# An attention and FFN layer on eight cores: 53 tiles of exponentials on VectorE in place of 43, and a new planner of the order of work

## The reference, cut to what matters

```python
# x: 4 x 4096 x 1024; 16 heads of queries (64 wide), one head of keys and values
x = x + attention(layernorm(x))
x = x + ffn(layernorm(x))

def attention(r):
    q = einsum('bnd,hkd->bnhk', r, query_proj)
    k = r @ key_proj                       # one key head for all 16
    v = r @ value_proj
    sim = einsum('bnhk,bmk->bnhm', q, k) / sqrt(64)
    o = einsum('bnhm,bmv->bnhv', softmax(sim), v)
    return einsum('bnhv,dhv->bnd', o, output_proj)

def ffn(x):
    s = x @ Win + bin_                     # 1024 -> 64
    h = relu(s[..., None] * W1 + b1)       # 16 per unit
    g = sum(h * W2, -1) + b2
    return g @ Wout + bout
```

## Time and profile before

| | |
|---|---|
| median of three runs | 975.62 us |
| the profiled execution, its own time | 975.78 us |
| its span, slowest core | 974.2 us |
| spans of the eight cores | 972.4 to 974.2 us |
| ScalarE busy | 913.7 us, 94% |
| TensorE matmul busy | 896.4 us, 92% |
| VectorE busy | 649.2 us, 67% |

### The profile page before, as it was taken

How to read it: one execution, slowest core, us unless ns; L and a number is a source line. 1 busy time by engine, 2 the same in 40 slices (tenths; PEclk the granted TensorE clock), 3 DMA queues, 4 the chain that set the end, 5 groups by cost and what they waited for, 6 DMA issues and landing times.

```text
span 974.2 us, 29152 instructions; the slowest of 8 cores (972.4 to 974.2 us)
## 1 busy us (share of the span) xinstructions
PE 896.4 (92%) x11484; PEld 479.6 (49%) x11484; DVE 649.2 (67%) x938; ACT 913.7 (94%) x1000; POOL 77.0 (8%) x150
## 2 busy tenths in 40 slices
PE   4799899999999999999999999999999998998884
PEld 3345555555445545554555455554544454444441
DVE  4545666662438987878888878778852368828725
ACT  2579999999999999999999999999999999999971
POOL 3201121220000001000010000000010000100000
PEclk9999999999999999999999999999999999999995
DMA  9602244550110200000130000100040010421101
GB/s 208 139 14 88 89 107 119 125 132 2 21 26 8 26 9 13 19 7 7 51 130 14 18 18 13 18 8 28 30 136 18 18 24 7 134 64 18 50 2 43
DMA packets 46291, 48.71 MB, mean 50 GB/s; under 512 B 35152, under 2 KB 35280, under 8 KB 46160
## 3 DMA queue, kind: packets, MB, share of 16 engines
q1 hardware_dynamic: 38352, 27.71, 11.1%
q0 software_dynamic: 7520, 18.62, 7.4%
q10 hardware_dynamic: 288, 0.52, 0.1%
HBM read 35.70 MB, written 8.39 MB: 45 GB/s over the span
## 4 chain that ended last, share of the span: by engine, by line
ACT 81%; issue 11%; PE 4%; DVE 2%; DMA 1%; POOL 0%; DVEq 0%; SPq 0%; POOLq 0%; ACTq 0%
ACT ptu L1082 81%; PE ob L646 1%; DMA xbuf<-x_own 1%; DVE lnst L668 0%; PE spa L911 0%; DVE lnst L672 0%; PE sdb L579 0%; PE spb L948 0%; PE spb L911 0%; POOL rstd L1105 0%; DVE qt L745 0%; DVE r1u L691 0%; ACT hz L1092 0%; PE sda L568 0%; DVE gacc L1052 0%
## 5 line engine op out<-in xcount | busy, mean ns | idle before, releaser
L1082 ACT ACTIVATE ptu<-spa 128x1024 bf16<-128x1024 f32 x491 | 560.3, 1141 | 15.9 <-PE spa L911 15.5
L1082 ACT ACTIVATE ptu<-spb 128x1024 bf16<-128x1024 f32 x490 | 560.6, 1144 | 0.6 <-PE spb L911 0.5
L646 PE MATMUL ob<-vab,ptu 128*128 128x65 bf16 x7848 | 390.5, 195 | 1.0 <-DVE vab L742 0.6
L646 PEld LDWEIGHTS ob<-vab,ptu 128*128 128x128 bf16 x7848 | 285.4, 97 | 199.5 <-issue 199.5
L911 PE MATMUL spa<-qt,k2t 64*128 64x512 bf16 x982 | 192.9, 381 | 26.4 <-ACT ptu L1082 17.8
L911 PE MATMUL spb<-qt,k2t 64*128 64x512 bf16 x980 | 192.2, 380 | 20.7 <-ACT ptu L1082 19.4
L911 PEld LDWEIGHTS spa<-qt,k2t 64*128 64x128 bf16 x982 | 57.9, 92 | 116.1 <-issue 103.3
L911 PEld LDWEIGHTS spb<-qt,k2t 64*128 64x128 bf16 x980 | 59.0, 92 | 112.8 <-issue 99.4
L978 DVE TENSOR_TENSOR oacc<-oacc,ob 128x520 f32<-128x520 f32 x52 | 36.2, 696 | 71.7 <-PE ob L646 71.3
L1103 POOL TENSOR_SCALAR lnve<-lnmv 128x1 f32<-128x1 f32 x48 | 17.9, 374 | 561.1 <-DVE lnmv L674 561.1
L841 DVE SCALAR_TENSOR_TENSOR r1t<-oacc 128x1024 bf16<-128x1024 f32 x43 | 52.6, 1224 | 5.6 <-DVE oacc L836 5.2
(11 more groups left out here) (139 smaller groups left out, 729.1 us busy)
## 6 DMA issues: line engine op xcount, KB each, us to landing
xbuf<-x_own SPq DMA_DIRECT2D x16, 512.0 KB, 5.8
xbuf<-x_oth SPq DMA_DIRECT2D x16, 512.0 KB, 3.8
out<-xbuf POOLq DMA_DIRECT2D x14, 512.0 KB, 3.0
xbuf<-x_own POOLq DMA_DIRECT2D x12, 512.0 KB, 7.2
wqb<-wq POOLq DMA_DIRECT2D x8, 256.0 KB, 6.3
xtra<-x_own SPq DMA_DIRECT2D x4, 512.0 KB, 4.8
xtra<-wp POOLq DMA_DIRECT2D x8, 256.0 KB, 4.5
ot<-on SPq DMA_TRANSPOSE x38, 2.3
```

The costliest lines, as they stand in the source:

```text
L646: r = te.matmul(osum[:, hd, c * 65:(c + 1) * 65], ptu[:, g % NPT, hd * 512 + c * 128:hd * 512 + (c + 1) * 128], vab[:, CHUNKS[s][i], :], s ...
L1082: sc.activation(ptu[:, g % NPT, :], sps[g % 2][:], AF.Exp, scale=0.125 / SCORE_SCALE).then_inc(ex, 1)
```

## The change

1. `OFF` takes 53 tiles from ScalarE, in place of 43: 19, 19 and 15 for k = 1, 2, 3, in place of 17, 17 and 9. The last segment has four, where it had one.
2. `pace` is written anew. It keeps a clock for each engine and a time for every exponential (`exp_at`), plays VectorE's streams in order of time by priority, and lets a TensorE piece in only if it ends before the next scores are due. VectorE has six streams: `out_side` (was `o_out`) and `key_norm_side` (the norms of tiles 4 to 31, which were part of the evacuations) are added, and its block now just follows one list `order`.
3. The opening: `phase_a_order` has the queries of pairs 1 and 2 before the transposes; the statistics of tiles 2 and 3 come one norm earlier; ScalarE doubles `wkb` after its first copy, not before; one query weight is loaded a tile earlier.

```diff
-OFF = {1: [1, 2, 3, 2, 3, 2, 2, 2], 2: [2, 2, 3, 2, 2, 2, 2, 2], 3: [2, 0, 0, 2, 1, 2, 1, 1]}
+OFF = {1: [2, 3, 2, 3, 2, 2, 2, 3], 2: [2, 3, 4, 3, 2, 2, 1, 2], 3: [2, 1, 1, 3, 1, 0, 3, 4]}
...
-    o = [("V", 0, 0)] + q(0, 1) + tr[:1] + q(0, 2) + tr[1:2] + q(0, 3) + tr[2:3] + q(0, 4) + tr[3:]
-    o += [("V", 1, 0)] + q(0, 5, 6, 7)
+    o = [("V", 0, 0)] + q(0, 1, 2) + tr[:2] + q(0, 3) + tr[2:] + q(0, 4) + [("V", 1, 0)] + q(0, 5, 6, 7)
...
-SWITCH = 20
+SWITCH = 10
...
+MARGIN = 4
...
+    def run_dve(w):
+        clock["dve"] = max(clock["dve"], ready_at(head[w][0])) + head[w][1]
+        order.append(w)
         head[w] = next(sides[w], None)
...
+            force(want, "s")
+            clock["pe"] = max(clock["pe"] + SWITCH * (mode[0] != "halves"), exp_at[g] + EXPED)
+            exp_at[g + 2] = max(exp_at[g + 1] + SLOT, clock["pe"] + SCORED)
+            clock["pe"] += SCORES
...
+            off = [j for j in range(done["epv"], len(OFF_TILES)) if OFF_TILES[j][0] == s]
+            if off and not (6 <= r and ok([("exv", off[0] + 1)], clock["pe"]) or r >= n - 1 - len(off)):
+                off = []
+            off_at[g] = off[:1]
+            force(want + [("exv", j + 1) for j in off[:1]], "v")
...
+            limit = exp_at[g + 2] + SLOT - SCORED - MARGIN if g + 2 in exp_at else 1 << 40
...
+            end = start + PIECE + SWITCH * (mode[0] != ("whole" if whole else "halves")) + SWITCH * whole
+            if g + 3 < NG and not open_end:
+                limit = max(limit, ready_at(wanted(g + 3)) - 2)
+            if end > limit and not (open_end and start <= clock["pe"]):
+                break
...
         def _(v):
 
             ln_stats(v, 0)
             ln_stats(v, 1)
             ln_norm(v, 0)
+            ln_stats(v, 2)
             ln_norm(v, 1)
-            ln_stats(v, 2)
+            ln_stats(v, 3)
             ln_norm(v, 2)
-            ln_stats(v, 3)
             ln_norm(v, 3)
...
+            for w in order:
+                next(sides[w], None)
...
-            sc.wait_ge(wkl, 16)
-            sc.activation(wkb[:, :, 64:128], wkb[:, :, 0:64], AF.Copy).then_inc(wkd, 1)
...
+                if step == 0:
+                    sc.wait_ge(wkl, 16)
+                    sc.activation(wkb[:, :, 64:128], wkb[:, :, 0:64], AF.Copy).then_inc(wkd, 1)
...
-                for c in {2: [1], 3: [2], 4: [3], 5: [4], 6: [5], 7: [6], 8: [7]}.get(i, []):
+                for c in {2: [1], 3: [2, 3], 4: [4], 5: [5], 6: [6], 7: [7]}.get(i, []):
```

391 lines of the change are left out of this document (222 added, 169 removed).

## The result

The change makes the kernel slower: 980.1 us (median), beside 975.7 before; the ratio of after to before is **1.0046, with a 95% interval of 1.0032 to 1.0061**. Forecast were 972.9 us. 980.1 lies just inside the range given, on the wrong side of no change.

The account below looks back on a forecast made before the run. ScalarE was taken to set the pace at 0.919 us per exponential, besides the opening and the end. From the profiled 975.78: -9.2 + 1.5 - 8.2 - 1.8 + 14.8 = -2.9, so 972.9 us, range 965.5 to 981.

Parts of the forecast that it names:

- Ten exponentials, -9.2: ScalarE gets 971 tiles in place of 981, at 0.919 us each: 9.2 us less if ScalarE stays the bound.
- From k = 1 on, +1.5: From k = 1 on, VectorE's added load makes some evacuations late: 1.5 us more, between zero and 11.
- nothing prices one: From k = 1 on: the old trace has no late evacuation, so their cost was taken between zero and 11 us.
- the 4 at which it called itself wrong: From k = 1 on: at most 2 us of ScalarE waits on scores expected; wrong if more than 4.
- The opening, -8.2: Up to exponential 16: earlier start and fewer waits put it at 47.3, from 55.55, 8.2 us less.
- the walk: Step-by-step reckoning of TensorE and VectorE through the first 16 slots: first exponential near 24.5, then waits of 8.1 us.
- thinnest margin: In the opening, the second of five query-weight loads issued earlier must land by 27.9 us.
- Near 100 us, -1.8: Near 100 us: a 1.4 wait and 0.4 of short steps go, as slab 2's keys finish two slots earlier.
- The end, +14.8: Behind X, the last exponential's start: late off tiles put `zrec` at X + 16.1, 14.3 us more, plus 0.5 for the clock.
- I take 0.5 us for that: In the end: cost allowed for TensorE's clock falling while it is nearly idle for six us, 0.5 us.
- Rival (a): In the end: clock down when the last off tile is ready, costing 1.3 and 1.2 more, 974.9 us; chance 0.12.
- Against: it did work until X + 5: In the end: argument against (a), that TensorE worked until 5 us after the last exponential's start, X.

Follow-up runs that it names:

- e8: The changed kernel with each tile of x asked for again as soon as its own store is done, not after the group's last: 979.0 us.
- e7: The changed kernel with the scores computed twice in slots from k = 1 on where TensorE has nothing else: 980.9 us.
- e2: The changed kernel with the old table of 43 off tiles, so the new planner and opening alone: 969.9 us.
- e4: The changed kernel with 12 and 30 unread matmuls on TensorE ahead of its waits for the last two off tiles' exponentials: 977.3 us.

## Why the prediction was wrong, by its steps

- **Ten exponentials, -9.2: right.** The pace stayed 0.919, and VectorE at 89% in k = 1 and 2 held no one back. A tile cost VectorE 6.7 us (66.7 for ten) and not 7.6.
- **From k = 1 on, +1.5: measured +3.2 on the slowest core, +1.9 on the mean, by another mechanism.** That the mean is close is luck. It counted late evacuations; there are none. The step that failed is "nothing prices one": the costs were a load on GpSimd's queue that VectorE waits for (e8) and TensorE's clock in slots with scores alone (e7). The order had shown 20 such slots for 7, and the prediction counted only the fullest slots, never the emptiest. It also laid this term to the ten tiles, and e2 loses as much without them. The view of waits has 3.0 us, more than the 2 it expected and less than the 4 at which it called itself wrong.
- **The opening, -8.2: measured -7.9, right in size,** number 16 at 47.64 for 47.3. On this core two errors cancel, which is luck: the first exponential starts 2.2 earlier than the walk had it, and the waits behind it are 10.6 and not 8.1. The seven groups of TensorE ahead of the values take 3.6 us (17.19 to 20.81), where the walk gave each of them up to 0.85. Such a group of eight matmuls is busy for 0.61 us from there on, and for 1.01 to 1.06 in the profiled core of before up to 23.07, which looks like the two levels of the clock. The means of the cores (-1.5 for the start, -6.2 for the waits) are near the walk's -1.6 and -6.7. The walk gave 2.9, 1.5 and 3.7 for three waits; they are 2.9, 2.0 and 3.8, and number 1 waits 1.65, which it did not have. It called the landing of the second query weights its thinnest margin. Late were those of pair 1 (1.66 on this core), a load that the change doesn't move: it moves the piece that needs them forward.
- **Near 100 us, -1.8: measured -0.35.** The old wait did go, and a new one at number 20, 1.49 us for the values of slab 1, took its place on all eight cores. The step said only what becomes earlier and not what is late next.
- **The end, +14.8: measured +17.9, +17.2 on the mean. This is the term that failed most.** Its order of events was right to 0.2 us up to the end of the first late polynomial (X + 2.9 for X + 2.7), and at full clock right to 0.5 us as far as the reciprocal (e4). The failed step is "I take 0.5 us for that", the clock: up to the reciprocal it costs 2.2 on the mean and 2.7 on core 4. With the walk's 14.3, its own 0.5 and 0.2 behind the reciprocal, 2.2 gives the 17.2. Rival (a), which said the clock is down when the last tile is ready, had 0.12 and was true on all eight cores. That its price of 2.5 is near is partly luck. It had 1.3 for the last six pieces and 1.2 for the product and the tail. The product and the pieces together cost 1.3, and the tail hardly anything. The other 0.9 lay further ahead, in the first eight "op" pieces, which neither the forecast nor (a) saw at the lower clock. "Against: it did work until X + 5" was no reason: TensorE was busy for 0.39 us from 929 to 932, and at 932 the clock was down on core 4.
- **The sum.** -2.9 forecast, +3.6 found in the spans: four errors of 0.3, 1.4, 1.7 and 3.1, all to the slow side. The forecast was moreover a small difference of large terms: 19.2 us less against 16.3 more. The profiled execution is the fastest of its kernel, 979.31 for a median of 980.1; the profiled one of before, 975.78, was at its median.

By the Trainium skill, "TensorE: Matmul & The Clock Gate", section "What's actually happening", throttled is the array's default state and activity releases it. e4 and e7 agree with it: products that change no result take the clock from 0.50 to 1.00 in the end and from 0.79 to 1.00 in k = 1. The same section says that the gate watches activity in a rhythm of its own, which a kernel's start does not reset. That would fit that the light slots cost 1.2 us on some cores of one execution and nothing on others; no run here isolates it.

Open is why the wait at number 887 differs so much from core to core, 0 to 3.0 us in one execution of e7. That the late reload is its cause is shown by e8; what makes one reload later than another wasn't tried.

## What to carry to other kernels

Work moved off the bounding engine is worth its pace only while something else still covers it: price each piece by where its last dependent step falls, and treat the last segment as another kernel. Here a tile earns 0.92, the third in the last head cost 2.2 and the fourth 13.7. Where several engines follow a fixed order, look in the new order for its emptiest slots as well as for its fullest, and for every piece that moves forward ask when the load it needs was issued. And a table and the planner that reads it are one change: under the old planner the same ten tiles cost 78 us.
